# A decoder layer with routed experts: three token scatters under way at a time instead of two

## What is computed

```python
x = x + attention(layernorm(x))              # 16 heads, latent keys and values
x = x + cross_attention(layernorm(x), ctx)   # 64 context rows a batch
xf = layernorm(x)                            # 2048 tokens of 256
shared = (silu(xf @ Sg) * (xf @ Su)) @ Sd
probs = softmax(xf @ Wr)                     # 16 experts
topk_p, topk_i = top_k(probs, 2)             # two experts a token
routed = sum over the token's experts e of
         topk_p * (silu(xf @ Wg[e]) * (xf @ Wu[e])) @ Wd[e]
x = x + routed + shared
```

## Time and profile before

| | us |
|---|---|
| median of 3 runs | 595.67 |
| lowest and highest of them | 595.23 and 597.32 |
| the profiled execution | 600.31 |
| its span from the first to the last instruction | 598.6 |

### The profile page before, as it was taken

How to read it: one execution, slowest core, us unless ns; L and a number is a source line. 1 busy time by engine, 2 the same in 40 slices (tenths; PEclk the granted TensorE clock), 3 DMA queues, 4 the chain that set the end, 5 groups by cost and what they waited for, 6 DMA issues and landing times.

```text
span 598.6 us, 14095 instructions
## 1 busy us (share of the span) xinstructions
PE 542.4 (91%) x4519; PEld 293.4 (49%) x4520; DVE 375.1 (63%) x1001; ACT 392.8 (66%) x568; POOL 212.7 (36%) x238
## 2 busy tenths in 40 slices
PE   3985999999999999999999899999997989999960
PEld 2452333333333333333336677767564567777740
DVE  5797556556657655565554478877876654444564
ACT  4477989899999999999993455554443373333310
POOL 4000693297019800000003243280356624555550
PEclk9998999999999999999998999999989899999995
DMA  9933334444444444444414730000012234444846
GB/s 253 364 114 67 62 71 75 76 79 78 76 78 76 79 78 76 78 76 79 82 42 139 199 88 2 2 1 2 2 61 88 88 107 126 141 141 141 278 151 211
DMA packets 53596, 60.20 MB, mean 101 GB/s; under 512 B 10770, under 2 KB 44691, under 8 KB 53555
## 3 DMA queue, kind: packets, MB, share of 16 engines
q1 hardware_dynamic: 46546, 46.19, 32.6%
q0 software_dynamic: 3792, 10.36, 4.9%
q10 hardware_dynamic: 3216, 3.15, 1.5%
HBM read 22.17 MB, written 18.61 MB: 68 GB/s over the span
## 4 chain that ended last, share of the span: by engine, by line
PE 74%; DVE 10%; SPq 4%; ACT 4%; issue 3%; DMA 3%; DVEq 1%; another core or an unknown queue 1%; POOL 0%; ACTq 0%; POOLq 0%
PE ps L715 19%; PE ps L726 19%; PE ps L1113 8%; PE ps L1130 3%; PE ps L994 3%; PE ps L859 2%; PE ps L759 2%; PE ps L927 2%; SPq L412 2%; SPq L414 2%; PE ps L1007 2%; PE ps L1105 2%; DVE ftmp L1787 2%; PE ps L642 2%; DMA qT<-y_tok 1%
## 5 line engine op out<-in xcount | busy, mean ns | idle before, releaser
L1646 DVE TENSOR_TENSOR ps<-ps,kstack 128x128 f32<-128x128 f32 (+3 forms) x256 | 123.1, 492 | 97.9 <-PE ps L715 97.4
L1269 ACT ACTIVATE pT<-ps 128x1024 f32<-128x1024 f32 x128 | 125.0, 1034 | 6.4 <-PE ps L715 3.5
L715 PE MATMUL ps<-qstack,kstack 96*128 96x512 bf16 x352 | 93.0, 387 | 6.4 <-ACT kstack L1258 3.9
L726 PE MATMUL ps<-pT,vcur 128*32 128x256 f32 x1024 | 80.5, 387 | 0.0
L1269 ACT ACTIVATE xn<-ps 128x1024 f32<-128x1024 f32 x64 | 65.8, 1028 | 7.7 <-PE ps L715 7.5
L1269 ACT ACTIVATE xnT<-ps 128x1024 f32<-128x1024 f32 x64 | 65.9, 1030 | 0.7 <-PE ps L715 0.5
L592 POOL DMA_INDIRECT y_tok<-ftmp,dest_i x47 | 45.1, 959 | 51.7 <-DVE ftmp L2065 50.2
L715 PEld LDWEIGHTS ps<-qstack,kstack 96*128 96x128 bf16 x352 | 27.4, 98 | 65.1 <-issue 31.3
L1113 PE MATMUL ps<-parts,xnT 128*128 x188 | 52.5, 402 | 3.0 <-issue 2.5
L565 POOL TENSOR_TENSOR resid<-resid,projb 128x512 f32<-128x512 f32 x8 | 10.1, 1267 | 114.6 <-DVE xn L1980 114.0
L1446 ACT ACTIVATE oT<-ps 128x128 f32<-128x128 f32 x47 | 13.0, 277 | 54.3 <-PE ps L1113 48.6
(11 more groups left out here) (296 smaller groups left out, 944.4 us busy)
## 6 DMA issues: line engine op xcount, KB each, us to landing
qstack<-parts SPq DMA_DIRECT2D x132, 64.0 KB, 2.3
x_slots<-wcur SPq DMA_DIRECT2D x1, 6016.0 KB, 20.8
kT<-x_slots SPq DMA_DIRECT2D x47, 128.0 KB
kstack<-parts SPq DMA_DIRECT2D x132, 32.0 KB, 2.0
early<-parts SPq DMA_DIRECT2D x60, 64.0 KB, 2.3
resid<-in_x_dram SPq DMA_DIRECT2D x4, 512.0 KB, 6.7
parts<-in_L_ffn_Wg_dram SPq DMA_DIRECT2D x16, 128.0 KB, 2.3
parts<-in_L_ffn_Wu_dram SPq DMA_DIRECT2D x16, 128.0 KB, 2.3
```

Of the source, the lines that this page charges most:

```text
L715: nc.tensor.matmul(ps[:, score_bank(g3, kt) + g, :], kstack[g3][:, kt * P:(kt + 1) * P], qstack[g3][:, 1 - first, 512 * g:512 * (g + 1)], ...
L726: mm = nc.tensor.matmul(out_g, vcur[:, r, kt, :], pT_ring[kt % 4].rearrange("p (t g q) -> p g t q", g=4, q=2 * HD)[:, g, :, :], start=(kt ...
L1269: nc.scalar.activation(pT_ring[kt % 4], two_banks(score_bank(g3, kt)).rearrange("p a n -> p (a n)"), ACT.Exp, bias=-SHIFT).then_inc(s_exp, 1)
L1646: nc.vector.tensor_tensor(blk, blk, within[:, side, 4 * P - n:] if side == 0 else within[:, side, 0:n], ALU.mult)\
```

## The change

POOL waits for scatter n - 3 instead of n - 2. The semaphores, their number and all other engines' instructions stay as they were; PE, DVE, ACT and SP have the same instructions in the same order, and POOL has the same instructions less one wait (the third scatter has none now). Since the four semaphores go round with n, scatter n - 3 is still the last one that raised its semaphore when POOL waits for it.

```diff
@@ -581,8 +581,8 @@
                     pool.wait_ge(s_place, TOPK * g + r + 1)
                     for t in range(HALF * g, HALF * (g + 1)):
                         n = HALF * (TOPK * g + r) + t % HALF
-                        if n > 1:
-                            pool.wait_ge(s_scatter[(n - 2) % 4], 16 * ((n - 2) // 4 + 1))
+                        if n > 2:
+                            pool.wait_ge(s_scatter[(n - 3) % 4], 16 * ((n - 3) // 4 + 1))
                         nc.gpsimd.indirect_dma_start(x_slots, bass.IndirectOffsetOnAxis(ap=place_i[:, r, t:t + 1], axis=0),
                                                      xe[:, t, :], None).then_inc(s_scatter[n % 4], 16)
```

## The result

| | before | with three at a time |
|---|---|---|
| median of 6 runs each, us | 597.16 (595.23 to 599.83) | 607.32 (605.51 to 609.72) |
| ratio to before | | 1.0156 [1.0127, 1.0184] |
| profiled execution, its span, us | 600.31, 598.6 | 607.98, 606.2 |
| last scatter begins, us | 483.76 | 485.06 |
| first transposes of slot tiles, us | 488.96 | 497.46 |

The change made the kernel 1.6% slower. The predicted 595.7 us and the range up to 598.2 are both wrong, and even the 602.3 of the slower rivals is not enough. Some executions came over 1.5% longer than the fastest of their kernel, the profiled one of the last experiment (e14) among them, and the ratios leave these out.

The account below looks back on a forecast made before the run. PE was taken as the bound, busy 542.4 of 598.6 us, with no scatter on its path. POOL's 2.3 us counted as 0 there: 600.31 + 0 = 600.31, carried over to the median 595.7 us; range 593.3 to 598.2.

Parts of the forecast that it names:

- the slower rivals: Stalls beside the scatters lengthened, DVE held up or scatters later: 599 to 602.3 us, 12% together.
- What POOL does: POOL's scatters near the 1.26 us floor, one landing late: last start about 481.4, 2.3 us earlier.
- The base: Profiled execution 600.31 us, 4.64 above the median of the runs shown; zero change carried over to 595.7 us.
- 0 us on the path: At the first slot-tile transposes PE comes later than the loads, so earlier scatters gain 0, at most 0.14 us.
- The rival that the stalls belong to the scatters, with the other sign: Three scatters lengthen a stall like DVE's ahead of `places`: 599.3 us alone, 602.3 with the slow clock; 8%.
- The clock: After a longer PE idle, the granted clock stays at its lower level as long again: up to 3.0 us.
- both signs: DVE's stalls beside the scatters lessened, 589.1 to 592.4 us, 11%; or lengthened, 599.3 to 602.3, 8%.
- DVE and POOL in each other's way: Short DVE operations in `places` and behind delayed by scatter issues: 597.0 us, or 599.5 at whole issues; slower 2%.
- The scatters don't get closer: Landings take as much longer as issues come earlier: last start stays 483.76, time 595.7 us, 12%; slower that way 2%.

Follow-up runs that it names:

- e14: Kernel before with three scatters allowed in the second half only, two in the first, on chip 7: 603.35 us, ratio 1.0089.
- e13: Three allowed, the seventh scatter of the first half held until the second half's count has come, on chip 7: 611.83 us, 1.0204 against the kernel before.
- r4: The changed kernel, three at a time, run again unchanged on chip 15: 593.25 us, ratio 0.9918 to the kernel before.
- e8: Kernel before with three scatters allowed in the second half only, two in the first, on chip 15: 594.38 us, ratio 0.9945.
- e12: Kernel before with three scatters allowed in the second half only, two in the first, on chip 6: 594.95 us, ratio 0.9951.
- e5: Kernel before with the wait between scatters removed entirely, so no limit, on chip 7: 607.21 us, ratio 1.0132.
- the held kernel: Three allowed, the first half's seventh scatter held until the second half's count; against the kernel before 598.84 and 600.07 us on chip 6, 611.83 on chip 7.
- r1: The kernel before, run again unchanged on chip 7: 597.22 us in one execution.

## Why the prediction was wrong, point by point

- **What POOL does.** Right in kind: the floor of 1.26 us, waits for landings of 0.9 us at three places. The first half's last start was forecast at 457.0 and came at 456.21, its run being 1.1 us early. The second half took 19.6 us, forecast 20.1. But its start was taken as fixed at 461.32, and it was 465.50: that is the step in which the stalls entered. Last start 485.06 instead of 481.4.
- **The base.** The forecast of no change was tied to 595.7, a median of three runs; over six runs the kernel before took 597.2, so 1.5 us of the miss are the base.
- **Who waits for POOL: 0 us on the path.** True of the trace it was read from, and after it too L1105 follows L1077 without a gap. As a statement about the kernel it is wrong. In that trace PE was late at L1105 because of the stalls, and this lateness hid the scatters. On chip 15 PE waits 6.0 us for the load in the kernel before, and the same change takes 4.7 us off (593.25 against 597.98).
- **The rival that the stalls belong to the scatters, with the other sign.** This was the mechanism. It had 8% and a price of 3.6 to 6.6 us; the trace gives 8.5 up to L1105. The terms that were mis-sized: I took one more stall of 3.0 to 3.6 us; it was 3.5 more at the count and 1.2 at the cast, partly covered, together 4.2 on PE, and besides a third stall of 3.5 us at the silu, which I had not thought of because it has no like on the path of the kernel before. Off the path it had one: ACT's silu at 461.14 was of the kind "remote" too and came 2.5 us behind its matmuls (455.07 + 3.60). The clock was put at up to 3.0 for as long again; it was 1.7 for the last `down` less 0.9 elsewhere. Against this rival I had held that no stall begins or ends with a scatter's issue or landing. For the one trace I had, that was so. After the change the stall at the count ends 2.43 us behind the last issue of the first half and the third one 2.2 us behind the last of all, and e13 shows that the stalls at the cast and the count go when the scatters beside them go.
- **Why its weight was too small.** The profile had named no cause for 3.57 us on the chain, right beside the resource that the change presses harder. An unexplained stall there is a reason to widen the range to its side, and I gave both signs about the same.
- **DVE and POOL in each other's way.** L1880 took 0.23 us after the change, when no issue ran beside it (none between 457.2 and 465.5), against 0.43 in the earlier trace rows; L1885 0.17 in both. In e14 the same operation beside an issue took 0.47. My reading that L1885 is not touched was wrong: what counts is when in the issue an operation starts. In r4 it is L1885 that is slow (DVE, POOL):

```profile
451.20 0.41 DVE L1885 TENSOR_SCALAR shift<-shift 128x16 f32<-128x16 f32 x1
```
```profile
450.67 0.96 POOL L586 DMA_INDIRECT x_slots<-val,place_i  x1 [0.30 <-issue]
```

  In all twenty traces, each of the two operations that starts 0.47 to 0.69 us into an issue ends 0.93 to 0.95 us into it and so takes 0.24 to 0.47 us; those that start 0.01 to 0.14 us into it, or 0.79 us, take their 0.17 or 0.23 us as without a scatter. So the Trainium skill's page "SBUF — State Buffer", section "Who interferes with whom", which says that the two engines share ports, is borne out for both operations, but its rule that the first comer keeps them for its whole instruction is not: the price was at most 0.24 us, and L1885 ran freely at the start of an issue of 0.96. Nothing in the result hangs on it.
- **The scatters don't get closer.** False everywhere: with three allowed they stand 1.26 us apart but for single gaps, on all chips.
- **Two at a time, then three** (e14, e8, e12) is the mildest of the versions: 0.4 to 0.55% faster on chips 6 and 15, 0.9% slower on chip 7. No version I ran is faster than the kernel before on both kinds of chip, and on chips with the stalls the kernel before is the best of them.

**What stays open.** Why chip 7 (and whichever ran the first two traces) holds releases and chips 6 and 15 do not. Whether the number under way or the pace matters was not told apart, since e5, without a limit, has the pace of three. Half the bytes ran only where there are no stalls. Each chip came up once or twice, and only the held kernel puts the stalls themselves to a test on chip 7, with one trace and two timed executions. One candidate is the recording itself, as every run here was recorded: held releases and missing records come together. The Trainium skill's page "NOTIFIC — the notification-queue block", section "7.1 Overflow: three behaviours, one of which stalls the engine", says that the block which writes such records can, depending on how it is set, discard them when a queue is full, or hold up the engine that produces them. Its authors never saw a queue overflow in what they measured. The traces here show both symptoms, but no run here shows that one causes the other; the recording is no part of the kernel, and no run without it was made.

## What to carry to other kernels

A wait that a profile gives no cause for, on the path and beside the resource that you are about to load more, belongs in the sum with a size and a sign, and not among the oddities: find out first whether it is there on another chip too. "Nobody waits for this" is a statement about one trace; ask what would be late if the engine in front of it were on time. Indirect DMAs issued without a pause can hold back what other engines are waiting for, so a change that packs them closer is to be timed on several chips, and beside its own kernel before on each.

## What the runs showed of the hardware that I had not expected

- The same two programs compare as 1.0156 and 1.0165 on one occasion each and as 0.9918 on chip 15, while the kernel before takes 597 to 599 us on all of them. In it the two effects nearly cancel: with stalls PE is late and waits 0 or 2 us (r1) for the tiles, without stalls it is early and waits 6 us for them.
- Releases of PE were held for up to some 20 us (e13: matmuls done at about 466.5, ACT at 486.17). In trains without a pause they were let go 2.0 to 3.3 us after the last scatter's issue had ended, at the count 2.43 to 2.46 us after it in four traces out of four.
- An indirect DMA of 128 rows mostly occupied POOL for 0.96 us with a gap of 0.30 us (the first of a kernel for 1.31, single ones for up to 2.17), whether a row has 256 columns or 128, and whether two, three or any number may be under way.
- A short DVE operation (L1880, L1885) that started 0.47 to 0.69 us into such an issue ended 0.93 to 0.95 us into it, up to 0.24 us late; one that started 0.01 to 0.14 us into it was not held.
